# A turn's split products in one run and its transposes, expert products and values in another

## The chip, the cores and the metric

The kernel runs on one core of one Trainium2 chip. The time is that of one execution on the device, in microseconds (us); the figure given for a kernel is the median of its runs. TensorE multiplies matrices and transposes tiles, ScalarE applies functions and copies, VectorE does elementwise work and reductions, GpSimd small elementwise work, and SyncE (SP) issues the DMA transfers. Each engine takes its own instructions in order and waits on semaphores that others raise.

## The reference, cut to what matters

Eight sequences of 512 tokens and 256 features pass two layers. The part in question is the first layer's attention (16 heads of 64) together with its expert network:

```python
q = rmsnorm((xn @ Wq).reshape(B, T, H, D), q_rms_w)
k = rmsnorm((xn @ Wk).reshape(B, T, H, D), k_rms_w)
v = (xn @ Wv).reshape(B, T, H, D)
gate = softplus(einsum('bthd,hd->bht', k, u_n) / sqrt(D))
bias = -dist * omega_eff[head] * gate[b, head, j]          # causal
attn = softmax(q @ k.T / sqrt(D) + bias)
x = x + (attn @ v) @ Wproj + experts(xn)    # 32 experts, 8 tokens of each sequence for each
# experts: h = gelu([merged, 1] @ w1[e]); o = [h, 1] @ w2[e]
```

## The kernel before

The attention runs in 64 **turns**; turn s is one sequence and one pair of heads. The turns are a software pipeline written out by hand: in turn s TensorE makes the **scores** of s, transposes the softmax weights of s - 1 (**p**, ten 128x128 blocks for each of the two heads, turn_p0 and turn_p1), multiplies them with v (**values** of s - 1), turns q, k and the bias terms of s + 1 (turn_q, turn_k, turn_aug) and **projects** s + 2 in four pieces of six products (project(s + 2, 0) to (s + 2, 3)).

Scores and projections are **split products**: each operand is held as a high and a low part in the fp32r type, and three products of parts make one. Transposes, values and the expert products are plain fp32.

Every two turns of four begin an expert (s mod 4 is 0 or 1: `hidden`, its first product, and add_bias), the next two end it (s mod 4 is 2 or 3: `turn_hidden`, `expert_output`). In s mod 4 = 2 ScalarE first computes the Gelu of two experts, with a table load before and one after. After every eighth turn TensorE multiplies a whole sequence with Wproj (L1050), 11.4 us.

All eight PSUM banks are in use: bQ (two, pieces of a projection in turn), bR (three) and bS (three). Scores fill bS and bR; the first head's p goes over bS, the second's over bR; values and expert products take bS[0] and bS[1], turn_hidden takes bS[2], which is also the bank of the third group of p0; q, k and the bias terms are turned in bR. So who has copied what out of a bank decides when the next may write.

The other engines, in a turn, in their order before the change:
- ScalarE: square(s + 1); exps of four score tiles (or Gelu); copies of p0 (groups 0 and 2); **rsqrt**(s + 1), an Ln and an Exp; takes piece 1 of the projection; copies of p1; exps; gate (Exp, Ln); takes piece 2; exps; copy_y; copies of q, k and bias terms; takes piece 3.
- VectorE: **lows**, the reductions of the scores (each raises `maxed`; the last four come after mean_square); takes piece 0; copy_p0; newton_step; copy_p1; copy_hidden; gate_input, norm, gate; divide; and the low parts.
- GpSimd: **augment**(s + 1), six small operations that make the slopes and shifts that turn_aug transposes, from gate's result.

The chain that the text speaks of is: square -> mean_square -> rsqrt -> newton_step -> gate_input and norm -> gate -> augment -> turn_aug -> copy_aug -> scores of the next turn. Lines of the rows: L939 scores, L978 transposes of p, L926 project, L1006 values, L1017 and L1034 expert products, L1025 turn_hidden, L959, L964 and L970 turn_q, turn_k and turn_aug; on ScalarE L1201 the copies of p, L1160 and L1163 the Ln and Exp of rsqrt, L1192 exps, L1175 copy_q; on VectorE L1348 lows, L1293 take_raw, L1304 the first Newton step, L1322 gate, L1388 copy_hidden.

## Time and profile before

| what | us |
|---|---|
| median of 3 runs (lowest to highest) | 1359.23 (1357.82 to 1359.45) |
| span of the profiled execution | 1353.4 |
| TensorE busy in the span | 1309.2 |
| VectorE busy | 1090.3 |
| ScalarE busy | 947.7 |
| GpSimd busy | 190.3 |
| first scores of turn 0 to first scores of turn 63 | 86.9 to 1065.7 |

The span runs from the first to the last instruction of the one execution that was profiled; what lies around it (start and end of the launch) is not in it, so the runs' times are some 6 us longer. A matmul in the trace is shown with its modelled end; consecutive ones overlap, so what a run of them costs is read from start to start. Where rows are merged ("x10"), the time is from the first start to the last end. "[0.67 <-POOL ag L1491]" says how long the engine stood idle before and whose event ended it.

### The profile page before, as it was taken

How to read it: one execution, taken by the hardware profiler on the slowest of the kernel's cores; microseconds unless marked ns; L12 is line 12 of the kernel's file. 1: busy time of each engine (PE TensorE's matmuls, PEld its weight loads, DVE VectorE, ACT ScalarE, POOL GpSimd, SP SyncE). 2: the span in 40 equal slices, each digit the busy share in tenths (PEclk: the TensorE clock that was granted, in tenths of full speed). 3: DMA queues.
4: the chain of work that ended last, by engine and by line, in shares of the span. 5: the costliest groups of instructions: out<-in, count | busy, mean ns of one | idle time of the engine just before them, and what ended most of it. 6: DMA issues, size and time to landing. Idle time of an engine off the chain costs nothing. (4 is left out here: it accounts for less than half of the span.)

```text
span 1353.4 us, 32125 instructions
## 1 busy us (share of the span) xinstructions
PE 1309.2 (97%) x11499; PEld 1103.9 (82%) x11499; DVE 1090.3 (81%) x3337; ACT 947.7 (70%) x2376; POOL 190.3 (14%) x564
## 2 busy tenths in 40 slices
PE   5899999999999999999999999999999799999999
PEld 3688888887978888797888878888888588888888
DVE  6869996999699789969996998799699867777663
ACT  6759885888588678858885887688598724444333
POOL 4512111111011111101111111111111100000000
PEclk8889999999999999999999999999999999999999
DMA  6452231332323222322322233233232322111100
GB/s 216 171 173 88 73 132 59 110 116 74 102 74 131 80 89 87 104 88 88 119 93 92 84 102 109 67 108 103 77 99 72 108 82 62 55 56 55 55 17 32
DMA packets 90831, 125.17 MB, mean 92 GB/s; under 512 B 8761, under 2 KB 77105, under 8 KB 90673
## 3 DMA queue, kind: packets, MB, share of 16 engines
q1 hardware_dynamic: 90352, 123.11, 28.2%
q8 instruction: 93, 1.52, 0.5%
q14 instruction: 66, 0.53, 0.1%
q10 hardware_dynamic: 320, 0.00, 0.0%
HBM read 103.69 MB, written 19.40 MB: 91 GB/s over the span
## 5 line engine op out<-in xcount | busy, mean ns | idle before, releaser
L1192 ACT ACTIVATE prob<-prob,low 128x512 f32<-128x512 f32 (+3 forms) x512 | 280.8, 551 | 115.7 <-DVE low L1348 115.7
L1348 DVE CUSTOM_DVE_ANT_0 prob<-at,mask 128x512 f32<-128x512 f32 (+3 forms) x512 | 219.6, 485 | 10.3 <-PE at L939 10.3
L926 PE MATMUL at<-w_hi,c_lo 128*128 128x386 f32 x512 | 190.1, 371 | 1.5 <-DVE area_raw L1293 1.5
L926 PE MATMUL at<-w_hi,c_hi 128*128 128x386 f32 x512 | 174.3, 340 | 0.0
L926 PE MATMUL at<-w_lo,c_hi 128*128 128x386 f32 x512 | 174.0, 340 | 0.0
L1361 DVE TENSOR_SCALAR prob<-prob,rec 128x512 f32<-128x512 f32 (+3 forms) x512 | 169.3, 394 | 4.5
L978 PE MATMUL at<-ident,prob 128*128 128x128 f32 x1280 | 164.3, 275 | 3.2 <-DVE low L1348 1.8
L1006 PE MATMUL at<-probT,v 128*32 128x512 f32 (+3 forms) x2048 | 152.6, 438 | 3.8 <-DVE probT L1371 2.6
L978 PEld LDWEIGHTS at<-ident,prob 128*128 128x128 f32 x1280 | 142.4, 140 | 10.6 <-DVE yT_lo L1377 1.6
L1006 PEld LDWEIGHTS at<-probT,v 128*32 128x32 f32 x2048 | 67.3, 110 | 89.8 <-issue 80.7
L1201 ACT ACTIVATE probT<-at 128x512 f32<-128x512 f32 (+1 forms) x256 | 130.3, 536 | 4.4 <-PE at L978 1.5
L1479 POOL TENSOR_TENSOR slope<-gl,omega 128x8 f32<-128x8 f32 x64 | 12.8, 200 | 842.8 <-DVE gl L1322 821.9
L1149 ACT ACTIVATE area_raw<-at 128x386 f32<-128x386 f32 x192 | 93.4, 486 | 21.6 <-PE at L926 19.5
L926 PEld LDWEIGHTS at<-w_hi,c_lo 128*128 128x128 f32 x512 | 97.3, 190 | 2.2 <-DVE area_raw L1293 1.8
L926 PEld LDWEIGHTS at<-w_lo,c_hi 128*128 128x128 f32 x512 | 97.6, 191 | 0.1
L926 PEld LDWEIGHTS at<-w_hi,c_hi 128*128 128x128 f32 x512 | 96.8, 189 | 0.0
L1192 ACT ACTIVATION_READ_ACCUMULATOR prob<-prob,low 128x1 f32 x512 | 96.7, 189 | 0.0
L939 PE MATMUL at<-kT_hi,qT_hi 64*128 64x512 f32 (+3 forms) x512 | 86.6, 331 | 6.6 <-ACT kT_hi L1179 6.6
L939 PE MATMUL at<-kT_lo,qT_hi 64*128 64x512 f32 (+3 forms) x512 | 85.1, 326 | 1.5
L939 PE MATMUL at<-kT_hi,qT_lo 64*128 64x512 f32 (+3 forms) x512 | 84.7, 324 | 0.0
L939 PE MATMUL at<-kaug,qaug 64*128 64x512 f32 (+3 forms) x512 | 83.6, 319 | 0.0
L1297 DVE TENSOR_REDUCE ssq<-area_sq 128x16 f32<-128x1024 f32 x64 | 77.7, 1214 | 1.6 <-ACT area_sq L1156 1.6
(254 smaller groups left out, 3195.9 us busy)
## 6 DMA issues: line engine op xcount, KB each, us to landing
area_w<-in_L_ffn_w SPq DMA_DIRECT2D x65, 1024.0 KB, 5.5
bias<-in_L_ffn_w SPq DMA_DIRECT2D x160, 32.0 KB, 4.4
x_in<-in_L_attn_x SPq DMA_DIRECT2D x8, 512.0 KB, 5.5
xr<-in_L_attn_x SPq DMA_DIRECT2D x8, 512.0 KB, 4.6
eo_d<-hidT SPq DMA_DIRECT2D x32, 128.0 KB, 1.8
x_d<-xr SPq DMA_DIRECT2D x8, 512.0 KB, 2.9
area_raw<-x_d SPq DMA_DIRECT2D x8, 512.0 KB, 3.9
out<-area_raw SPq DMA_DIRECT2D x7, 512.0 KB, 3.1
```

Of the source, the lines that this page charges most:

```text
L926: m = eng.matmul(bQ[n % 2][:, 0:W], a[:, (j // HP) % 2, k, n * P:(n + 1) * P], w[:, k, j % HP, :], start=start, stop=(k == KC - 1 and a is ...
L939: m = eng.matmul(bC[i][:, at:at + (c + 1) * P], q[rows, c * P:(c + 1) * P], k[rows, 0:(c + 1) * P], start=ready is k_hi_done, stop=q is qaug)
L978: m = eng.transpose(bP[h][i][:, at:at + P], prob[s % 2][h][:, off[c] + kc * P:off[c] + (kc + 1) * P], ident[:, :])
L1006: m = eng.matmul(bY[rows, kc * P:T], v[:, s % 2, kc, rows], probT[j * E // D][:, offT[kc]:offT[kc + 1]], start=(kc == 0), stop=(kc == NT - 1))
L1149: eng.activation(raw[:, j % 2, n, :], bQ[n % 2][:, 0:W], ACT.Copy).then_inc(raw_A.sem, 1)
L1192: eng.activation(sl, sl, ACT.Exp, scale=-1.0, bias=low[:, i:i + 1], accum_out=den[:, i:i + 1]).then_inc(exp_done.sem, 1)
L1201: eng.activation(probT[h][:, x:y], bP[h][i][:, 0:y - x], ACT.Copy).then_inc(done.sem, 1)
L1297: eng.tensor_reduce(ss[:, :], sq[:, :, :].rearrange("p n (i d) -> p (n i) d", d=D), AX.X, ALU.add).then_inc(ssd.sem, 1)
L1348: eng.tensor_tensor_reduce(out=prob[s % 2][h][:, off[c]:off[c + 1]], in0=bC[i][:, at:at + (c + 1) * P], in1=mask[:, (NT - 1 - c) * P:T], s ...
L1361: p = eng.tensor_scalar(sl, sl, rec[:, k:k + 1], None, ALU.mult)
L1479: eng.tensor_tensor(slope32[:, :, :], gl[:, :, :], omega[:, hp * 2:hp * 2 + 2].unsqueeze(1).to_broadcast([P, NT, 2]), ALU.mult).then_inc(a ...
```

## The change

TensorE's, ScalarE's and VectorE's programs of a turn are written in another order. No instruction is added or taken away.
- TensorE: the scores are followed by pieces 0 and 1 of the projection, then come all twenty transposes of p, the expert product, values, turn_q, turn_k, turn_aug, and then pieces 2 and 3. turn_hidden goes ahead of p0, and the third group of p0 now waits for copy_hidden. expert products go ahead of values.
- ScalarE: all four copies of p together, behind the take of piece 1; rsqrt behind them; the take of piece 2 at the end of the turn.
- VectorE: copy_hidden ahead of the copies of p; both copies of p together ahead of newton_step; take_raw (piece 0) behind gate.

```diff
--- before.py
+++ after.py
@@ -983,6 +983,8 @@
                 def turn_p0(s):
                     eng.wait_ge(p_done.sem, p_done.at(s, 1))
                     for i in range(3):
+                        if i == 2 and ends_in(s + 1) is not None:
+                            eng.wait_ge(hidT_done.sem, hidT_done.at(ends_in(s + 1)))
                         if s + 1 < NTURN:
                             eng.wait_ge(maxed.sem, maxed.at(s + 1, i + 1))
                         turn_p(s, 0, i)
@@ -1019,7 +1021,7 @@
                     p.then_inc(pe_h.sem, 1)
 
                 def turn_hidden(m, s):
-                    eng.wait_ge(pt0_A.sem, pt0_A.at(s - 1))
+                    eng.wait_ge(maxed.sem, maxed.at(s, 3))
                     eng.wait_ge(hid_done.sem, hid_done.at(m // 2))
                     for f in range(NF):
                         p = eng.transpose(bH[:, f * P:(f + 1) * P], hid[:, m % 2, f * P:(f + 1) * P], ident[:, :])
@@ -1102,8 +1104,6 @@
                     else:
                         eng.wait_ge(y_done.sem, y_done.at(s - 2))
                         eng.wait_ge(eo_done.sem, eo_done.at(E - 1))
-                    if s > 0:
-                        turn_p0(s - 1)
                     if s + 2 < NTURN:
                         eng.wait_ge(o_done.sem, o_done.at((s - 1) // HP - 1))
                         project(s + 2, 0)
@@ -1111,19 +1111,18 @@
                     if s + 2 < NTURN:
                         project(s + 2, 1)
                     prepare(s, 1)
-                    if s > 0:
-                        turn_p1(s - 1)
                     if ends_in(s) is not None:
                         turn_hidden(ends_in(s), s)
-                    if s + 2 < NTURN:
-                        project(s + 2, 2)
-                    prepare(s, 2)
                     if s > 0:
-                        values(s - 1)
+                        turn_p0(s - 1)
+                        turn_p1(s - 1)
                     if begins_in(s) is not None:
                         hidden(begins_in(s), s)
                     if ends_in(s) is not None:
                         expert_output(ends_in(s), s)
+                    prepare(s, 2)
+                    if s > 0:
+                        values(s - 1)
                     if s + 1 < NTURN:
                         if s == 0:
                             eng.wait_ge(maxed.sem, maxed.at(0, 8))
@@ -1131,6 +1130,7 @@
                         turn_k(s + 1)
                         turn_aug(s + 1)
                     if s + 2 < NTURN:
+                        project(s + 2, 2)
                         project(s + 2, 3)
                     prepare(s, 3)
                     if 0 < s < NTURN and s % HP == 0:
@@ -1244,18 +1244,17 @@
                     elif s < NTURN:
                         exps(s, 3)
                         exps(s, 1)
-                    if s > 0:
-                        copy_p(s - 1, 0, 0)
-                        copy_p(s - 1, 0, 2)
                     prepare(s, 0)
-                    if s + 1 < NTURN:
-                        rsqrt(s + 1)
                     if s + 2 < NTURN:
                         take_raw(s + 2, 1)
                     prepare(s, 1)
                     if s > 0:
+                        copy_p(s - 1, 0, 0)
+                        copy_p(s - 1, 0, 2)
                         copy_p(s - 1, 1, 0)
                         copy_p(s - 1, 1, 2)
+                    if s + 1 < NTURN:
+                        rsqrt(s + 1)
                     if s % 4 == 2:
                         exps(s, 3)
                         gate(s + 1)
@@ -1264,8 +1263,6 @@
                         exps(s, 2)
                     if s + 1 < NTURN and s % 4 != 2:
                         gate(s + 1)
-                    if s + 2 < NTURN:
-                        take_raw(s + 2, 2)
                     prepare(s, 2)
                     if s < NTURN:
                         exps(s, 0)
@@ -1280,6 +1277,7 @@
                         copy_k(s + 1)
                         copy_aug(s + 1)
                     if s + 2 < NTURN:
+                        take_raw(s + 2, 2)
                         take_raw(s + 2, 3)
                     prepare(s, 3)
                 second.scalar(eng)
@@ -1434,22 +1432,21 @@
                     if s < NTURN:
                         lows(s, 2)
                         lows(s, 0)
-                    if s + 2 < NTURN:
-                        take_raw(s + 2)
+                    if ends_in(s) is not None:
+                        copy_hidden(ends_in(s))
                     prepare(s, 0)
+                    prepare(s, 1)
                     if s > 0:
                         copy_p(s - 1, 0)
-                    prepare(s, 1)
+                        copy_p(s - 1, 1)
                     if s + 1 < NTURN:
                         newton_step(s + 1)
-                    if s > 0:
-                        copy_p(s - 1, 1)
-                    if ends_in(s) is not None:
-                        copy_hidden(ends_in(s))
                     if s + 1 < NTURN:
                         gate_input(s + 1)
                         norm(s + 1)
                         gate(s + 1)
+                    if s + 2 < NTURN:
+                        take_raw(s + 2)
                     if s < NTURN:
                         divide(s, 0)
                     if begins_in(s) is not None:
```

TensorE, in the middle of a turn that begins an expert, before, from the second head's transposes of p (L978) over a piece of the projection (L926) and values (L1006) to the expert product (L1017):

```order
L978 MATMUL at<-ident,prob 128x128 x10
L926 MATMUL at<-w_hi,c_lo 128x386
L926 MATMUL at<-w_lo,c_hi 128x386
L926 MATMUL at<-w_hi,c_hi 128x386
L926 MATMUL at<-w_hi,c_lo 128x386
L926 MATMUL at<-w_lo,c_hi 128x386
L926 MATMUL at<-w_hi,c_hi 128x386
L1006 MATMUL at<-probT,v 32x512 x4
L1006 MATMUL at<-probT,v 32x384 x4
L1006 MATMUL at<-probT,v 32x256 x4
L1006 MATMUL at<-probT,v 32x128 x4
L1017 MATMUL at<-area_w,tok 32x256 x8
```

The same place after the change (L1019 is `hidden`, L1008 values), up to the first product of the third piece:

```order
L926 MATMUL at<-w_hi,c_hi 128x386
L978 MATMUL at<-ident,prob 128x128 x20
L1019 MATMUL at<-area_w,tok 32x256 x8
L1008 MATMUL at<-probT,v 32x512 x4
L1008 MATMUL at<-probT,v 32x384 x4
L1008 MATMUL at<-probT,v 32x256 x4
L1008 MATMUL at<-probT,v 32x128 x4
L959 MATMUL at<-ident,area_sq 128x128 x4
L964 MATMUL at<-ident,area_sq 128x128 x4
L970 MATMUL at<-ident,ag 68x128 x4
L926 MATMUL at<-w_hi,c_lo 128x386
L926 MATMUL at<-w_lo,c_hi 128x386
```

The piece that stood between the transposes and values has gone behind turn_aug (L970), where twelve products of L926 now stand ahead of the scores instead of six.

ScalarE in such a turn, before, from the second exps to the take of piece 2 (lnv and r are rsqrt; area_raw<-at is a take of a piece; probT<-at a copy of p; ge and gp are gate):

```order
L1192 ACTIVATE prob,dens<-prob,low 128x256 x2
L1201 ACTIVATE probT<-at 128x512
L1201 ACTIVATE probT<-at 128x384
L1160 ACTIVATE lnv<-ssq 128x16
L1163 ACTIVATE r<-lnv 128x16
L1149 ACTIVATE area_raw<-at 128x386
L1201 ACTIVATE probT<-at 128x512
L1201 ACTIVATE probT<-at 128x384
L1192 ACTIVATE prob,dens<-prob,low 128x384 x2
L1168 ACTIVATE ge<-ge 128x8
L1170 ACTIVATE gp<-ge 128x8
L1149 ACTIVATE area_raw<-at 128x386
```

After:

```order
L1192 ACTIVATE prob,dens<-prob,low 128x256 x2
L1149 ACTIVATE area_raw<-at 128x386
L1201 ACTIVATE probT<-at 128x512
L1201 ACTIVATE probT<-at 128x384
L1201 ACTIVATE probT<-at 128x512
L1201 ACTIVATE probT<-at 128x384
L1160 ACTIVATE lnv<-ssq 128x16
L1163 ACTIVATE r<-lnv 128x16
L1192 ACTIVATE prob,dens<-prob,low 128x384 x2
L1168 ACTIVATE ge<-ge 128x8
L1170 ACTIVATE gp<-ge 128x8
L1192 ACTIVATE prob,dens<-prob,low 128x128 x2
```

The two instructions of rsqrt moved from ahead of the second head's copies to behind them.

VectorE in a turn that ends an expert, after the change, behind its last reduction of the scores (L1346), up to divide:

```order
L1346 ISA prob,low<-at,mask 128x128
L1346 ISA low 128x1
L1386 COPY hidT<-at 128x256
L1369 COPY probT<-at 128x384 x2
L1302 SCALAR_TENSOR_TENSOR nw<-r 128x16
L1304 TENSOR_TENSOR nw<-nw,ssq 128x16
L1306 SCALAR_TENSOR_TENSOR rs<-nw,r 128x16
L1314 TENSOR_TENSOR gl<-area_raw,rs 128x8
L1316 SCALAR_TENSOR_TENSOR ge<-gl 128x8
L1324 TENSOR_TENSOR area_sq<-area_raw,rs 128x1024
L1320 SCALAR_TENSOR_TENSOR gl<-gl,gp 128x8
L1291 COPY area_raw<-at 128x386
```

copy_hidden (L1386) stood behind the second copy of p before, and the take of piece 0 (L1291) ahead of the first.

## Rows read from the trace of the kernel before

**Rows 1.** The page: span, busy time, granted clock in 40 slices, the group of p transposes.

```profile
span 1353.4 us, 32125 instructions
...
PE 1309.2 (97%) x11499; PEld 1103.9 (82%) x11499; DVE 1090.3 (81%) x3337; ACT 947.7 (70%) x2376; POOL 190.3 (14%) x564
...
PEclk8889999999999999999999999999999999999999
...
L978 PE MATMUL at<-ident,prob 128*128 128x128 f32 x1280 | 164.3, 275 | 3.2 <-DVE low L1348 1.8
```

**Rows 2.** The waits of TensorE, 200 to 1000 us: total, times, longest.

```profile
PE at L939 <- ACT kT_hi L1179: 4.0, 12, 0.5
```

**Rows 3.** The timeline of TensorE, turn 36: start, duration, engine, line, operation.

```profile
645.27 0.50 PE L939 MATMUL at<-kT_hi,qT_hi 64*128 64x512 f32 x2
...
647.99 1.31 PE L978 MATMUL at<-ident,prob 128*128 128x128 f32 x10
649.06 0.42 PE L926 MATMUL at<-w_hi,c_lo 128*128 128x386 f32 x1
649.32 0.34 PE L926 MATMUL at<-w_lo,c_hi 128*128 128x386 f32 x1
...
651.27 1.25 PE L978 MATMUL at<-ident,prob 128*128 128x128 f32 x10
...
657.68 0.60 PE L970 MATMUL at<-ident,ag 128*68 128x128 f32 x4
...
659.29 0.50 PE L939 MATMUL at<-kT_hi,qT_hi 64*128 64x512 f32 x2
```

**Rows 4.** The timeline of TensorE, first scores of turns 34 and 35.

```profile
616.15 0.50 PE L939 MATMUL at<-kT_hi,qT_hi 64*128 64x512 f32 x2
...
630.67 0.50 PE L939 MATMUL at<-kT_hi,qT_hi 64*128 64x512 f32 x2 [0.31 <-ACT kT_hi L1179]
```

**Rows 5.** The timeline of ScalarE in turn 36: rsqrt, copies of p1, exps.

```profile
650.79 0.21 ACT L1160 ACTIVATE lnv<-ssq 128x16 f32<-128x16 f32 x1
651.09 0.22 ACT L1163 ACTIVATE r<-lnv 128x16 f32<-128x16 f32 x1
...
651.91 1.15 ACT L1201 ACTIVATE probT<-at 128x512 f32<-128x512 f32 x2
652.95 0.61 ACT L1192 ACTIVATE prob<-prob,low 128x384 f32<-128x384 f32 x1
```

**Rows 6.** The timeline of turn 35: copy_q on ScalarE and VectorE's low part after it.

```profile
643.50 0.69 ACT L1175 ACTIVATE qT_hi<-at,q_scale 128x512 fp32r<-128x512 f32 x1 [0.83 <-PE at L959]
...
644.22 0.75 DVE L1333 SCALAR_TENSOR_TENSOR qT_lo<-at,q_scale,qT_hi 128x512 fp32r<-128x512 f32 x1 [0.32 <-ACT qT_hi L1175]
```

**Rows 7.** The timeline of VectorE in turn 0: take_raw, first Newton step, gate.

```profile
92.88 0.55 DVE L1293 COPY area_raw<-at 128x386 f32<-128x386 f32 x1
93.35 0.16 DVE L1304 SCALAR_TENSOR_TENSOR nw<-r 128x16 f32<-128x16 f32 x1
...
95.39 0.16 DVE L1322 SCALAR_TENSOR_TENSOR gl<-gl,gp 128x8 f32<-128x8 f32 x1
```

**Rows 8.** The timeline of TensorE: turn_aug of turn 0 and the first scores of turn 1.

```profile
97.49 0.63 PE L970 MATMUL at<-ident,ag 128*68 128x128 f32 x4 [0.67 <-POOL ag L1491]
...
99.11 0.49 PE L939 MATMUL at<-kT_hi,qT_hi 64*128 64x512 f32 x2
```

**Rows 9.** The timeline of turn 34: VectorE's gate and the last operation of augment.

```profile
625.88 0.16 DVE L1322 SCALAR_TENSOR_TENSOR gl<-gl,gp 128x8 f32<-128x8 f32 x1
...
627.52 0.21 POOL L1491 TENSOR_TENSOR ag<-shift,ag 128x8 fp32r<-128x8 f32 x1
```

**Rows 10.** The timeline of VectorE: copy_hidden in turn 35, first instruction behind lows in turn 36.

```profile
639.25 0.41 DVE L1388 COPY hidT<-at 128x256 f32<-128x256 f32 x1
...
651.36 0.56 DVE L1293 COPY area_raw<-at 128x386 f32<-128x386 f32 x1
```

**Rows 11.** Windows around turn 63: busy time of each engine, granted clock, DMA share.

```profile
1076.00:1079.50 3.50, 3.11 (x20) 1.05 (x24) 2.56 (x8) 1.60 (x7) 0.00 (x0) 0.51 0.00 0
```

## The prediction

> **What bounds the kernel now.** I read the page first: TensorE is busy 97% of the 1353.4 us span [rows 1]. "Busy" says little where matmuls are pipelined, so the second view is the list of waits, TensorE's own, in the stretch from 200 to 1000 us: in 800 us it waited 4.0 us in total [rows 2]. In these turns TensorE never stands still for long, so a turn lasts as long as its matmuls take. The other engines have slack, and what counts is how much of it a new order uses up.
>
> The third view is the timeline of a turn, from one first score product to the next [rows 3]: 645.27 to 659.29, 14.02 us, a turn that begins an expert (s mod 4 is 0 or 1). The turns that end one take 14.52 (616.15 to 630.67, the one with Gelu) and 14.60 (630.67 to 645.27) [rows 4]. I give times below from the turn's first score product.
>
> **The meant gain: fewer changes of kind.** Before, split products and plain fp32 work alternate three times a turn; after, once. What does a change cost? In [rows 3] the ten transposes begin at 647.99. A transpose follows the last one by 0.109 us (the run of ten lasts 1.25, one alone 0.275 [rows 1, 3]; nine steps are between), 0.16 after the first, so the tenth begins at about 649.03. The second product after it begins at 649.32, 0.29 later: one transpose step and one product step (0.109 + 0.177; the latter from 649.32 to 651.27, 11 steps). So the entry costs about nothing, and the exit into the transposes is one of these 11 equal steps. The first product's own step of 0.26 (649.06 to 649.32) against 0.177 bounds it from above: 0.08 an entry, two entries fewer in 61 turns, 10 us at most. Below nothing I have no reason for. I take 0, the value that the starts on both sides support. The changes between products on 128 rows, the scores on 64 and the 32-column products stay as many as they were.
>
> **The cost: the next turn's chain starts later and has one product piece more behind it.** It runs: last transpose of p1, ScalarE's copy of it, Ln and Exp of rsqrt (which the change puts behind all four copies), VectorE's Newton steps, gate input, norm and gate, GpSimd's six operations of augment, TensorE's turn_aug, then now two pieces of project instead of one, then the scores. Step by step for a turn that begins an expert:
> - Scores take 2.72 (645.27 to 647.99), the two pieces of project 2.21 (649.06 to 651.27) [rows 3]. So p0 begins at 4.93, and the last of the 20 transposes at 4.93 + 19 x 0.109 = 7.00. Before, the first p1 transpose began at 651.27 - 645.27 = 6.00, so p1 stands where it did, and p0 lies later.
> - From the last transpose's start to ScalarE's next instruction behind the copy: 652.95 - (651.27 + 9 x 0.109) = 0.70 [rows 3, 5]. Ln at 7.70. In the old order Ln came at 650.79 - 645.27 = 5.52, ahead of p1. This is the move that counts.
> - Ln to Exp 0.30, Exp 0.22 [rows 5], hop to VectorE 0.03 (643.50 + 0.69 to 644.22 [rows 6]): Newton at 8.25.
> - Newton to gate, with gate input and norm between, 2.04 (93.35 to 95.39) [rows 7]: gate at 10.29. These rows are from the first turn, the only place where TensorE already waits for augment: gate to turn_aug is 95.39 to 97.49, 2.10 [rows 7, 8]. While VectorE's big multiplications ran beside it, GpSimd was slower; in the turn at 616 VectorE stood idle first, and gate to GpSimd's last end was 627.73 - 625.88 = 1.85 [rows 9], 1.88 with a hop of 0.03. After the change a copy from PSUM (take_raw) stands behind gate, ahead of the multiplications. I take 1.95, nearer to the short one, and keep both. turn_aug at 12.24.
> - turn_aug to the scores with one piece behind it is 1.62 (97.49 to 99.11) [rows 8], one more piece is 6 x 0.177 = 1.06: next scores at 14.92. Before 14.02: **+0.90**.
>
> Does TensorE come earlier than 12.24? Before, from the end of p1 (651.27 + 10 x 0.109 = 652.36) to turn_aug (657.68) it took 5.32 with one piece in it, so without it 4.26: 7.11 + 4.26 = 11.37. It waits some 0.9 us before turn_aug, with the two pieces and the scores queued behind it. turn_q, eight transposes earlier (11.37 - 8 x 0.109 = 10.50), needs norm, which ends as gate starts, at 10.3: no wait of its own. The old turn_aug began at 657.68 - 645.27 = 12.41, so it hardly moves: the old slack of the chain paid for the later rsqrt, and the piece behind it is then bare.
>
> **Turns that end an expert.** turn_hidden now stands ahead of p0: 2 x 0.109 = 0.22. The third group of p0 waits for VectorE's copy of the hidden values (one PSUM bank). VectorE gets to it after the turn's last score reduction, 651.36 - 645.27 = 6.09; the copy takes 0.41, hop 0.03: 6.53 [rows 3, 10]. The group would be due at 4.93 + 0.22 + 7 x 0.109 = 5.91. A stall of 0.62, and all behind it later by 0.84: 15.76. Against 14.52 and 14.60: **+1.24** and **+1.16**. If VectorE is done sooner the stall could vanish; that is the low bound, 30 x 0.62 = 19 us. The Gelu turn has a second suspect: its scores already wait 0.31 for copy_k [rows 4], so copy_k ends at about 14.5. The exps ahead of it started when the p1 copies ended, at 7.8 (651.91 + 1.15 - 645.27 [rows 5]); now they start behind rsqrt, at 7.70 + 0.84 + 0.52 = 9.06. That puts copy_k at 15.8, less the take of a piece that has gone behind it: on the edge of 15.76, so I add nothing, and 0.2 in 15 turns for the range.
>
> **What costs nothing.** VectorE's and ScalarE's takes of the third piece move to the turn's end, where only the piece after next needs their bank. Values wait for all four copies, which end at 7.8; TensorE stands at 7.1 then with an expert's products between, which cover them. If they did not, values would be 0.7 late. The expert products run earlier in the turn; their weights are issued by the same SP instructions at a turn's end or start, a turn ahead, and the SP queue passes nothing new.
>
> **The sum.** Turns 1 to 61 carry all of it: 31 x 0.90 = 27.9, 15 x 1.24 = 18.6, 15 x 1.16 = 17.4. Turn 0 has no transposes of p; its chain begins 0.47 earlier (92.88 to 93.35, the copy ahead of Newton goes [rows 7]) and gets 1.06 behind it, less 0.15 for GpSimd: 0.5. The last turns have no projections; I put 0. Total 64.4: span 1353.4 to about 1418, and the median of the runs, which stands 5.8 above the profiled span, 1359.2 to **1424 us**.
>
> **Rivals.**
> - The gain is real and the wait is not (faster). If an entry costs the full 0.08 and the chain fits in TensorE's work, the time is 1359 - 10 = 1349. It decides if p1's last transpose to turn_aug takes under 11.37 - 7.00 = 4.4 us; the rows add up to 5.2. I see no hop that is 0.8 too long. 0.07 with all ways of being faster.
> - The wait is smaller than worked out, 1362 to 1395: half of the 0.9, no stall on the hidden copy. 0.06.
> - Nothing changes, since both are small: 0.02.
> - The clock falls. Transposes are now 20 or 22 in one run and twelve more stand around the new wait. The granted clock reads 9, so nine tenths or more, in each slice of the turns before [rows 1], but in 1076 to 1079.5, after a stretch of transposes with short waits, it was 0.51 [rows 11], which is 1.2 GHz. If each turn had such a stretch, 3.5 us at half the speed would lose up to 1.7 us, 61 times: 1424 + 104 = 1528. In the stretch before the fall there were several runs and three waits in 6 us; here some 2 us of transposes stand between products. 0.04.
> - The forecast, with its own range 1404 to 1442: 0.81.
>
> The Trainium skill, TensorE: Matmul & The Clock Gate, Part 4 (PE-mode transpose), says that transposes do not count as work for the clock as other matmuls do. By that rule the long run of transposes is the wrong thing to make, and the case of the falling clock would be the likeliest. The turns before, with 32 transposes in each and no slice of a lower clock, give it little room.
>
> **How the numbers follow.** The range: gate to turn_aug between 1.88 and 2.10 is -4 to +9 us, no hidden stall -19, copy_k +3, entries dearer than nothing -10, and 0.15 a turn for hops put together, +-9; not all at once, so 1404 to 1442. It leaves out the clock, most of the smaller wait and the faster cases, and the ends of my own: 2 in 10. This kernel's runs differ by 0.1%, so 0.2% is about what can be told from no change. Slower by more than that: 0.81 + 0.06 + 0.04 = 0.91; within 0.02; faster 0.07.
>
> **What would show it.** TensorE's waits should show turn_aug waiting for GpSimd's last augment operation in every turn, 0.8 to 1.1 us; waits at the third group of p0 for the hidden copy in 30 turns; turns of 14.9 and 15.8. Steps of products and transposes unchanged, clock 1.00. I am wrong if turns take under 14.0 (then changes of kind cost more than the starts show), or if the first wait is elsewhere, most likely at turn_q for norm or at the scores for copy_k.

## The result, and the profile after the change

The change makes the kernel slower: 1431.02 us (median of 4 runs, 1426.0 to 1434.0) against 1358.53 (4 runs, 1350.47 to 1359.45), a ratio of 1.0566 [1.0529, 1.0604]. This ratio and those below, each with its 95% interval, are the estimates on record and not the quotient of the two medians beside them, which would be 1.0534 here. The profiled execution spans 1429.6 us against 1353.4 [rows 1], so 76.2 more.

The page of the changed kernel, with the rows that answer to [rows 1] and the one of turn_aug (busy time, mean ns of one, idle time before and what ended most of it):

```profile
span 1429.6 us, 32157 instructions
...
PE 1330.6 (93%) x11499; PEld 1104.8 (77%) x11499; DVE 1100.6 (77%) x3337; ACT 973.4 (68%) x2376; POOL 193.3 (14%) x564
...
PEclk9799999999999999999999999999999989999999
...
L978 PE MATMUL at<-ident,prob 128*128 128x128 f32 x1280 | 158.8, 276 | 18.1 <-DVE hidT L1386 16.3
...
L970 PE MATMUL at<-ident,ag 128*68 128x128 f32 x256 | 40.6, 282 | 48.7 <-POOL ag L1488 48.7
```

The matmuls are the same 11499, and so are the counts of the other engines; the 32 instructions that the total has more are none of these. TensorE's share of the span fell from 97% to 93%; what is new is idle time ahead of two groups. The waits of TensorE from 200 to 1000 us, as in [rows 2] (total, times, longest):

```profile
PE at L970 <- POOL ag L1488: 37.0, 47, 0.9
PE at L978 <- DVE hidT L1386: 11.2, 24, 0.6
...
```

The first stands in every turn of the stretch, 47 in all, the second in each of its 24 turns that end an expert. The wait for copy_k, all that [rows 2] had, is not in the list any more. Now the timeline of TensorE in turn 33, which begins an expert (start, duration, tiles; compare [rows 3]):

```profile
642.23 0.50 PE L939 MATMUL at<-kT_hi,qT_hi 64*128 64x512 f32 x2
...
647.14 2.35 PE L978 MATMUL at<-ident,prob 128*128 128x128 f32 x20
649.42 1.07 PE L1019 MATMUL at<-area_w,tok 128*32 128x256 f32 x16
650.30 2.34 PE L1008 MATMUL at<-probT,v 128*32 128x512 f32 x32
652.65 0.66 PE L959 MATMUL at<-ident,area_sq 128*128 128x128 f32 x4
653.14 0.60 PE L964 MATMUL at<-ident,area_sq 128*128 128x128 f32 x4
654.53 0.63 PE L970 MATMUL at<-ident,ag 128*68 128x128 f32 x4 [0.79 <-POOL ag L1488]
...
657.21 0.50 PE L939 MATMUL at<-kT_hi,qT_hi 64*128 64x512 f32 x2
```

The turn lasts 14.98 us. turn_aug (L970) begins 1.88 after turn_q (652.65 to 654.53); in the turn of [rows 3] these two stand 0.93 apart. So the wait costs 0.95 from start to start, though 0.79 is listed: the listed figure counts from the modelled end of the matmul before. The chain that it waits for, in the same turn, on ScalarE (copies of p, Ln, Exp), then VectorE (first Newton step, gate), then GpSimd (last of augment):

```profile
647.84 2.18 ACT L1201 ACTIVATE probT<-at 128x512 f32<-128x512 f32 x4
649.91 0.21 ACT L1160 ACTIVATE lnv<-ssq 128x16 f32<-128x16 f32 x1
650.21 0.22 ACT L1163 ACTIVATE r<-lnv 128x16 f32<-128x16 f32 x1
```

```profile
650.46 0.18 DVE L1302 SCALAR_TENSOR_TENSOR nw<-r 128x16 f32<-128x16 f32 x1 [0.70 <-ACT r L1163]
...
652.51 0.16 DVE L1320 SCALAR_TENSOR_TENSOR gl<-gl,gp 128x8 f32<-128x8 f32 x1
```

```profile
654.15 0.33 POOL L1488 TENSOR_TENSOR ag<-shift,ag 128x8 fp32r<-128x8 f32 x1
```

VectorE stood idle for 0.70 before the Newton steps, so it was ScalarE's late Exp that set them; from there on each step of the chain began within 0.1 us of the end of the one before it. Then the two turns that end an expert, TensorE again: turn 34 (Gelu) from 657.21, turn 35 behind it from 672.86.

```profile
662.39 0.93 PE L978 MATMUL at<-ident,prob 128*128 128x128 f32 x7
663.68 1.64 PE L978 MATMUL at<-ident,prob 128*128 128x128 f32 x13 [0.37 <-DVE hidT L1386]
...
670.18 0.63 PE L970 MATMUL at<-ident,ag 128*68 128x128 f32 x4 [0.61 <-POOL ag L1488]
...
672.86 0.50 PE L939 MATMUL at<-kT_hi,qT_hi 64*128 64x512 f32 x2
...
678.26 0.93 PE L978 MATMUL at<-ident,prob 128*128 128x128 f32 x7
679.79 1.64 PE L978 MATMUL at<-ident,prob 128*128 128x128 f32 x13 [0.60 <-DVE hidT L1386]
...
686.47 0.63 PE L970 MATMUL at<-ident,ag 128*68 128x128 f32 x4 [0.79 <-POOL ag L1488]
...
689.16 0.50 PE L939 MATMUL at<-kT_hi,qT_hi 64*128 64x512 f32 x2
```

Both have two waits each; they last 15.65 and 16.30. After seven transposes of p the eighth, which is in the third group, waits for the copy of the hidden values. VectorE in turn 35, its first score reduction and that copy:

```profile
674.70 0.68 DVE L1346 CUSTOM_DVE_ANT_0 prob<-at,mask 128x512 f32<-128x512 f32 x1
...
679.32 0.42 DVE L1386 COPY hidT<-at 128x256 f32<-128x256 f32 x1
```

Not every such pair of turns is split like this one: in 7 of the 15 Gelu turns, turn_aug begins 2.16 behind gate instead of 1.84, they last 15.97 or more, and the turn behind them mostly 15.95 to 15.98. From turn 22 on the two together take 31.93 to 31.96 either way. In turn 34 GpSimd's fourth operation of augment took 0.21 and VectorE's four multiplications beside it 1.80; in turn 42, one of the longer ones, 0.51 and 1.41.

Turn 0 became longer by 1.3: 13.53 (86.37 to 99.90) for 12.25 (86.86 to 99.11). TensorE there, GpSimd's last operation of augment, and the windows of its transposes and of all full turns (busy time of PE, PEld, DVE, ACT and POOL, granted clock, DMA share, GB/s):

```profile
94.69 1.09 PE L959 MATMUL at<-ident,area_sq 128*128 128x128 f32 x4 [2.25 <-DVE area_sq L1324]
```

```profile
96.10 0.33 POOL L1488 TENSOR_TENSOR ag<-shift,ag 128x8 fp32r<-128x8 f32 x1
```

```profile
94.60:98.00 3.40, 3.31 (x15) 2.99 (x16) 3.37 (x10) 1.78 (x4) 2.29 (x8) 0.51 0.67 269
148.00:1125.00 977.00, 918.05 (x8618) 753.78 (x8620) 788.39 (x2494) 739.43 (x1899) 128.55 (x435) 1.00 0.28 88
```

With no values to make yet and the third piece gone behind, TensorE waited 2.25 us for norm, and the transposes after that wait ran at a granted clock of 0.51, the lower level of 1.2 GHz. In the full turns the clock is 1.00.

**The whole in one table.** The length of a turn is read from first score product to first score product, and is the mean over turns 4 to 61; "begin" are the turns that begin an expert and carry no output product, "output" those with the product of a sequence, "Gelu" s mod 4 = 2, "behind" s mod 4 = 3. The sum runs from the first scores of turn 1 to those of turn 62. The kernels e1 to e9 are the experiments below.

| kernel | begin | output | Gelu | behind | sum of turns 1 to 61 |
|---|---|---|---|---|---|
| before | 13.99 | 25.37 | 14.53 | 14.61 | 951.2 |
| after | 14.98 | 26.34 | 15.82 | 16.17 | 1024.8 |
| e1, rsqrt early | 14.18 | 25.53 | 15.01 | 15.71 | 980.8 |
| e2, piece 2 ahead | 14.02 | 25.91 | 15.54 | 15.53 | 985.5 |
| e3, hidden copy early | 14.98 | 26.32 | 15.35 | 15.80 | 1012.0 |
| e5 = e1 + e3 | 14.20 | 25.52 | 14.59 | 15.29 | 968.6 |
| e8 = e1 + e2 + e3 | 14.00 | 25.94 | 14.69 | 15.09 | 965.2 |
| e4, before with more changes of kind | 13.99 | 25.37 | 14.71 | 14.64 | 954.5 |
| e7, before with rsqrt late | 13.98 | 25.29 | 14.97 | 14.61 | 958.8 |
| e6, before with take 2 late | 13.99 | 25.37 | 14.15 | 14.61 | 945.5 |
| e9, e6 with exps late | 13.99 | 25.37 | 14.11 | 14.49 | 942.9 |

Of the 76.2 us, 73.7 stand in turns 1 to 61, 1.3 in turn 0, 0.5 in turn 62, 1.3 behind that, and the start took 0.5 less.

### The profile page after: what moved, and what is told of

Same layout as the page of the kernel before. It is cut to its first block and busy times, and to the rows that moved or that the text cites. A ratio compares the mean times of both kernels' runs of the same rounds, so it can differ in the third digit from the quotient of the medians.

```text
span 1429.6 us, 32157 instructions
## 1 busy us (share of the span) xinstructions
PE 1330.6 (93%) x11499; PEld 1104.8 (77%) x11499; DVE 1100.6 (77%) x3337; ACT 973.4 (68%) x2376; POOL 193.3 (14%) x564
## 5 line engine op out<-in xcount | busy, mean ns | idle before, releaser
L1346 DVE CUSTOM_DVE_ANT_0 prob<-at,mask 128x512 f32<-128x512 f32 (+3 forms) x512 | 220.1, 486 | 28.5 <-PE at L939 28.4
L926 PE MATMUL at<-w_hi,c_lo 128*128 128x386 f32 x512 | 185.6, 362 | 0.0
L978 PE MATMUL at<-ident,prob 128*128 128x128 f32 x1280 | 158.8, 276 | 18.1 <-DVE hidT L1386 16.3
L926 PE MATMUL at<-w_hi,c_hi 128*128 128x386 f32 x512 | 173.9, 340 | 0.0
L926 PE MATMUL at<-w_lo,c_hi 128*128 128x386 f32 x512 | 173.5, 339 | 0.0
L978 PEld LDWEIGHTS at<-ident,prob 128*128 128x128 f32 x1280 | 143.6, 142 | 27.1 <-DVE hidT L1386 23.9
L1201 ACT ACTIVATE probT<-at 128x512 f32<-128x512 f32 (+1 forms) x256 | 135.3, 545 | 35.5 <-PE at L978 31.9
L1008 PE MATMUL at<-probT,v 128*32 128x512 f32 (+3 forms) x2048 | 151.3, 436 | 0.0
L1008 PEld LDWEIGHTS at<-probT,v 128*32 128x32 f32 x2048 | 68.1, 110 | 84.6 <-issue 64.7
L1369 DVE COPY probT<-at 128x384 f32<-128x384 f32 x128 | 70.7, 554 | 43.4 <-PE at L978 42.7
L926 PEld LDWEIGHTS at<-w_hi,c_lo 128*128 128x128 f32 x512 | 96.6, 189 | 4.6
L926 PEld LDWEIGHTS at<-w_lo,c_hi 128*128 128x128 f32 x512 | 96.9, 189 | 0.1
L926 PEld LDWEIGHTS at<-w_hi,c_hi 128*128 128x128 f32 x512 | 96.5, 188 | 0.0
L970 PE MATMUL at<-ident,ag 128*68 128x128 f32 x256 | 40.6, 282 | 48.7 <-POOL ag L1488 48.7
```

The lines of the kernel that those rows point to most:

```text
L926: m = eng.matmul(bQ[n % 2][:, 0:W], a[:, (j // HP) % 2, k, n * P:(n + 1) * P], w[:, k, j % HP, :], start=start, stop=(k == KC - 1 and a is ...
L970: m = eng.transpose(bR[2][0:AG, n * P:(n + 1) * P], ag[:, n, :].bitcast(F32), ident[:, :])
L978: m = eng.transpose(bP[h][i][:, at:at + P], prob[s % 2][h][:, off[c] + kc * P:off[c] + (kc + 1) * P], ident[:, :])
L1008: m = eng.matmul(bY[rows, kc * P:T], v[:, s % 2, kc, rows], probT[j * E // D][:, offT[kc]:offT[kc + 1]], start=(kc == 0), stop=(kc == NT - 1))
L1201: eng.activation(probT[h][:, x:y], bP[h][i][:, 0:y - x], ACT.Copy).then_inc(done.sem, 1)
L1346: eng.tensor_tensor_reduce(out=prob[s % 2][h][:, off[c]:off[c + 1]], in0=bC[i][:, at:at + (c + 1) * P], in1=mask[:, (NT - 1 - c) * P:T], s ...
```

## The experiments

**Is it the late rsqrt?** e1 takes the changed kernel and puts rsqrt back ahead of the take of piece 1 and of ScalarE's copies of p; VectorE's order stays as changed.

```diff
                     prepare(s, 0)
+                    if s + 1 < NTURN:
+                        rsqrt(s + 1)
...
                         copy_p(s - 1, 1, 2)
-                    if s + 1 < NTURN:
-                        rsqrt(s + 1)
```

> The changed kernel with one edit: on ScalarE the Ln and Exp of rsqrt stand ahead of the take of piece 1 and of the four copies of p again. My theory (the chain to turn_aug is late because rsqrt waits for the last p1 copy, and it ends bare in front of two pieces): the chain then starts when VectorE has made its second copy of p, at about 7.5 us instead of 8.25 of a turn, and TensorE's wait at turn_aug falls from 0.8 to about 0.1 us; turns that begin an expert go from 14.98 to about 14.2, those that end one lose some 0.7 too; 1385 us in all (1378 to 1395). Rival (the long runs themselves cost, by the clock or by TensorE's steps): at most a few us are won, 1425 to 1431. Rival (VectorE, not ScalarE, holds the chain): Newton starts no earlier, 1431.

Measured: 1386.57 us (1381.67 to 1396.1), ratio 1.0256 [1.0193, 1.0319] to a before of 1353.09 in that comparison. TensorE's waits from 200 to 1000 us:

```profile
PE at L978 <- DVE hidT L1386: 11.7, 24, 0.6
```

The listed wait for augment is gone from all turns. It is not quite gone in time: TensorE in its turn 36,

```profile
675.28 0.66 PE L959 MATMUL at<-ident,area_sq 128*128 128x128 f32 x4
...
676.43 0.63 PE L970 MATMUL at<-ident,ag 128*68 128x128 f32 x4
```

turn_aug begins 1.15 after turn_q; in the kernel before, which also has plain fp32 work just ahead of turn_q, it is 0.93. So 0.22 is left, and the turns that begin an expert last 14.18, 0.19 more than before. Moving rsqrt back saves 44.0 of the 73.7 us; whether it is rsqrt's place alone that costs them, this run can't say.

**Is it the bare piece?** e2 leaves rsqrt late and puts piece 2 ahead of turn_q, where it covers the chain (VectorE's take_raw goes behind copy_hidden, so that piece 2 finds its bank free).

```diff
                         values(s - 1)
+                    if s + 2 < NTURN:
+                        project(s + 2, 2)
...
                         turn_aug(s + 1)
                     if s + 2 < NTURN:
-                        project(s + 2, 2)
                         project(s + 2, 3)
```

> The changed kernel with piece 2 of the projection ahead of turn_q (behind values) instead of behind turn_aug, and VectorE's take of piece 0 behind copy_hidden, which piece 2 needs; rsqrt stays late. My theory: the piece covers the wait at turn_aug, which falls from 0.8 to under 0.1 us, and turns that begin an expert go from 14.98 to 14.1; 1378 us (1370 to 1390). There is one more change of kind a turn; if those cost the upper bound of 0.08 us it is 5 us more. Rival (rsqrt's place alone makes the loss, whatever stands behind turn_aug): the wait at turn_aug stays and little is won, over 1415.

Measured: 1388.78 us (1385.19 to 1392.09), ratio 1.026 [1.0213, 1.0306]. Its waits from 200 to 1000 us:

```profile
PE at L978 <- DVE hidT L1387: 12.7, 24, 0.6
PE at L939 <- ACT kT_hi L1180: 6.2, 12, 0.8
PE at L1052 <- ACT area_raw L1150: 1.8, 6, 0.3
```

Turns that begin an expert are back at 14.02, with rsqrt as late as in the changed kernel. Putting the piece back saves 39.3 us, though rsqrt stays where it is. So the savings of e1 and e2 are not two shares of the loss: they take away the same wait, and the 0.98 needs both, a late chain and a piece that has left the place where it covered it. (A bare piece with the chain early still costs 0.19, as e1 shows.) What the changed kernel's longer Gelu turn hid comes up: the scores wait for copy_k, the prediction's second suspect, and the output product for a take on ScalarE.

**Is the late rsqrt alone harmful?** e7 is the other half: the kernel before with ScalarE's rsqrt behind its last copy of p, and VectorE's Newton steps behind both copies. TensorE's order is untouched.

```diff
-                    if s + 1 < NTURN:
-                        rsqrt(s + 1)
                     if s + 2 < NTURN:
                         take_raw(s + 2, 1)
...
                         copy_p(s - 1, 1, 2)
+                    if s + 1 < NTURN:
+                        rsqrt(s + 1)
```

> The kernel before with one part of the change alone: rsqrt behind all four copies of p on ScalarE and newton_step behind both copies on VectorE; TensorE's order is untouched. My theory (the late rsqrt only uses up the chain's slack; what costs is that the piece which covered it now stands behind turn_aug): gate at 10.3 us of a turn, turn_aug possible at 12.25 while TensorE comes at 12.4: turns stay within 0.1 us, 1353 to 1360. Rival (the late rsqrt alone costs what the change costs): 50 us more.

Measured: 1362.74 us (1356.9 to 1367.83), ratio 1.0062 [1.0033, 1.0091] to 1355.78. The turns that begin an expert do not move (13.98). Its waits from 200 to 1000 us, and the scores behind a Gelu turn:

```profile
PE at L939 <- ACT kT_hi L1179: 9.0, 12, 1.0
```

```profile
636.28 0.49 PE L939 MATMUL at<-kT_hi,qT_hi 64*128 64x512 f32 x2 [0.72 <-ACT kT_hi L1179]
```

Of the 7.6 us that the sum of turns rose, 6.9 stand in the 15 Gelu turns, where ScalarE reaches copy_k later still, and 1.3 in turn 3; the turns that begin an expert are 0.7 shorter together. The median lies above the 1353 to 1360 that I expected: I had not counted what the late rsqrt does to copy_k. For the turns that begin an expert it settles the prediction's sentence that the old slack of the chain paid for the later rsqrt: it did, and only the bare piece turned it into a wait.

**The hidden copy.** e3 lets VectorE copy the hidden values two reductions earlier, in the changed kernel.

```diff
                         lows(s, 2)
-                        lows(s, 0)
                     if ends_in(s) is not None:
                         copy_hidden(ends_in(s))
+                    if s < NTURN:
+                        lows(s, 0)
```

> The changed kernel with VectorE's copy_hidden ahead of the last two score reductions instead of behind them. My theory: TensorE's wait at the third group of p0 (0.37 and 0.60 us shown in the two turns that end an expert) nearly vanishes, and since the chain to turn_aug hangs on p1, all of it comes off these turns: 30 x 0.5 = 15 us, 1416 (1411 to 1422); turns that begin an expert stay at 14.98. Rival (the wait is only passed on, to the p1 groups that need the last reductions, or to turn_aug): 1428 to 1431.

Measured: 1416.42 us (1414.84 to 1420.6), ratio 1.0473 [1.0428, 1.0519]. Its waits:

```profile
PE at L970 <- POOL ag L1489: 36.8, 48, 0.9
PE at L978 <- DVE hidT L1386: 1.2, 7, 0.2
```

The stall at the third group fell from 11.2 to 1.2 in the list, the Gelu turn by 0.47 and the turn behind it by 0.37; the wait for augment stays.

**Do the two add up?** e5 has the edits of e1 and e3 together.

> The changed kernel with both edits, rsqrt early on ScalarE and copy_hidden ahead of the last two reductions. My theory (two separate losses, one in every turn, one in the turns that end an expert): the gains add, 1386 less 15: 1371 us (1365 to 1378). Rival (both take from the same slack): 1380 or more.

Measured: 1374.05 us (1372.74 to 1378.93), ratio 1.0136 [1.0094, 1.0178]. In sums of turns 1 to 61, e1 saves 44.0 and e3 12.8, together 56.8; e5 saves 56.2. They add up, so they are two waits at two places and not one that moves about.

**What is a change of kind worth?** e4 is the kernel before with the transposes of p cut into their groups and half pieces of the projection between them: six entries into split products in a turn instead of three, 183 more in turns 1 to 61.

```diff
+                    if mixed:
+                        turn_p0(s - 1, (0,))
...
+                        project(s + 2, 0, (0,))
+                        turn_p0(s - 1, (1,))
+                        project(s + 2, 0, (1,))
+                        turn_p0(s - 1, (2,))
+                        project(s + 2, 1, (0,))
+                        turn_p1(s - 1, (0,))
+                        project(s + 2, 1, (1,))
+                        turn_p1(s - 1, (1, 2))
```

> The kernel before with the same instructions, but the groups of p0 and the first of p1 alternate with halves of pieces 0 and 1: six entries from fp32 work into split products a turn instead of three, and six exits. 183 more of each in all. My theory (a change of kind costs nothing, by the starts on both sides): 1358 us, within 4. Rival (an entry costs the 0.08 us that its first product's step shows): 15 us more, 1373. If it were still more, the change's idea would be right and its price hidden by the new waits.

Measured: 1357.47 us (1351.2 to 1360.11), ratio 1.0029 [1.0002, 1.0055] to 1353.09. The turns that begin an expert last 13.99 as before. TensorE in one of them (L981 transposes of p, L928 project):

```profile
645.67 0.66 PE L981 MATMUL at<-ident,prob 128*128 128x128 f32 x4
646.08 0.42 PE L928 MATMUL at<-w_hi,c_lo 128*128 128x386 f32 x1
646.34 0.34 PE L928 MATMUL at<-w_lo,c_hi 128*128 128x386 f32 x1
646.52 0.34 PE L928 MATMUL at<-w_hi,c_hi 128*128 128x386 f32 x1
646.70 0.49 PE L981 MATMUL at<-ident,prob 128*128 128x128 f32 x3
646.94 0.42 PE L928 MATMUL at<-w_hi,c_lo 128*128 128x386 f32 x1
```

Three transposes (646.70 to 646.94) take 0.24, so 0.08 each where the step in a run is 0.109, and the first product behind them has a step of 0.26 where the next have 0.18. What the entry seems to cost is given back at the exit before it. Three more entries in a turn cost nothing that these turns show; the 3.3 us that the sum rose are in the Gelu turns (14.71), where copy_k is waited for longer (6.2 us in the list for 4.0).

**And with all the waits mended?** e8 is the changed kernel with e1's, e2's and e3's edits: one change of kind fewer in each turn than before, and no late chain.

> The changed kernel with all three: rsqrt early, piece 2 ahead of turn_q, copy_hidden early. Two runs of each kind a turn instead of three before, and none of the new waits. My theory (changes of kind are free): turns as before, 14.0, and 14.5 to 14.7 where an expert ends; within 5 us of the kernel before. Rival (a change of kind costs 0.08 us or more): 5 us or more faster than before, 0.996 and below.

Measured: 1365.27 us (1361.37 to 1376.54), ratio 1.007 [1.0043, 1.0098] to 1355.78. Its waits, and the third group of p0 in its turn 35:

```profile
PE at L1052 <- ACT area_raw L1150: 2.4, 7, 0.3
PE at L978 <- DVE hidT L1387: 2.0, 11, 0.2
```

```profile
650.39 0.93 PE L978 MATMUL at<-ident,prob 128*128 128x128 f32 x7
651.50 1.64 PE L978 MATMUL at<-ident,prob 128*128 128x128 f32 x13 [0.18 <-DVE hidT L1387]
```

The turns that begin an expert are at 14.00, those of before at 13.99: longer runs of one kind bring nothing even when nothing is late. I had expected the whole within 5 us of before, and it is 9.5 off by the medians, 14.0 by the sum of turns. Two rests make up nearly all of the 14.0. In the turns that end an expert, 15 x (0.16 + 0.48) = 9.6, the third group still comes late: in turn 35 the 13 transposes begin 1.11 behind the seven, where 7 x 0.109 = 0.76 would do, so 0.35 is lost, and in the Gelu turn 0.22 in the same way. And the seven output turns have 0.57 more each, 4.0, with the wait for a take on ScalarE in them.

**Mending the wait that the kernel before had.** The trace of before has one wait in its turns [rows 2], for copy_k in the Gelu turn. e6 lets ScalarE take piece 2 behind copy_aug there.

```diff
-                    if s + 2 < NTURN:
+                    if s + 2 < NTURN and s % 4 != 2:
                         take_raw(s + 2, 2)
...
                     if s + 2 < NTURN:
+                        if s % 4 == 2:
+                            take_raw(s + 2, 2)
                         take_raw(s + 2, 3)
```

> The kernel before with one edit: in the turns with a Gelu, ScalarE takes piece 2 of the projection behind its copies of q, k and the bias terms instead of ahead of the last exps, as the changed kernel does in every turn. There the scores of the next turn waited for copy_k (0.31) and then for VectorE's low parts. My theory: ScalarE's copies come 0.4 us earlier, the waits at the scores vanish, and the Gelu turn and the one behind it lose some 0.3 us each, 15 times: 5 to 9 us, 0.995 of before. Rival (ScalarE is late by its exps whatever the take's place): within 0.1%.

Measured: 1349.44 us (1343.32 to 1352.79), ratio 0.9952 [0.9926, 0.9979] to 1355.78. The Gelu turn went from 14.53 to 14.15 and TensorE has no wait listed from 200 to 1000 us. It ran a second time beside e9:

> The same kernel as with the late take of piece 2 alone, on the same chip as the one with both edits: 0.995 of before again, turns of 14.12 and 14.61.

Measured: 1350.51 us (1344.03 to 1356.15), and a before of 1350.46 in that comparison: ratio 1.000 [0.9977, 1.0022]. The turns are the same as the first time, so the kernel's own share is the 5.7 us of the sum of turns; the rest of a run varies more than that (last section). From the ratios alone, faster than before is not settled for e6: the second comparison does not bear the first out.

e9 adds to e6 that in Gelu turns ScalarE's last exps go behind copy_aug.

```diff
-                    if s < NTURN:
+                    if s < NTURN and s % 4 != 2:
                         exps(s, 0)
...
                         copy_aug(s + 1)
+                    if s < NTURN and s % 4 == 2:
+                        exps(s, 0)
```

> The kernel before with the late take of piece 2 in the Gelu turns and, in the same turns, ScalarE's last two exps behind its copies of q, k and the bias terms. What is left in the turn behind the Gelu turn (14.61 against 14.0 + 0.22 for turn_hidden) is the scores' third product waiting for VectorE's low part of k, which comes after ScalarE's copy of y. My theory: copy_y, copy_q and copy_k come some 0.6 us earlier, the low parts with them, and that turn goes from 14.61 to about 14.3: 4 to 5 us on top of the 6 of the late take, 0.992 of before. Rival (VectorE has no room: its own queue sets the low parts): the turn stays at 14.6 and the ratio at 0.995.

Measured: 1342.58 us (1339.46 to 1354.99), ratio 0.9946 [0.9918, 0.9974] to 1350.46. The turn behind Gelu fell from 14.61 to 14.49, less than the 14.3 hoped for. Its scores hardly wait any more, and p0 begins 0.33 earlier than in e6 (2.83 for 3.16 in turn 35), but half of that is lost at values, which begin 0.44 behind the last product ahead of them, for 0.27 in e6. The sum of turns is 8.3 us below before's. This kernel has the lowest median and the shortest turns of the study. Its ratio rests on one comparison, as e6's first did; what speaks for it beyond that is the sum of turns.

## Why the prediction was right, and where a size was off

1424 was forecast, 1404 to 1442, and 1431.02 came; slower, by the two waits that were named, at the two places named. The mechanism was right; that the number came so near is in part luck, some 4 us of it (see the step from span to median). By its steps:

- **Changes of kind are free.** Right: three more in a turn leave it at 13.99 (e4), one fewer at 14.00 (e8). The upper bound of 0.08 an entry would have been 0.24 for e4's turn, and is excluded.
- **The chain of a turn that begins an expert.** Forecast p0 at 4.93, Ln 7.70, gate 10.29, turn_aug 12.24, next scores 14.92; turn 33 shows 4.91, 7.68, 10.28, 12.30 and 14.98. The one step that was chosen between two rows, gate to turn_aug, was put at 1.95 and is 2.02 (652.51 to 654.53), nearer to the long end. The term measures 31 x 0.98 = 30.4 us for 27.9. e1 and e2 show that it was the late rsqrt and the bare piece together, as argued, and e7 that the first alone costs these turns nothing.
- **The hidden copy.** The mechanism is right (e3 takes it away); this is the mis-sized term of the sum. I had 15.76 for both turns, from VectorE's reductions ending 6.09 after the first scores. That figure came from turn 36, which begins an expert. It fits the Gelu turn: in turn 34 the eighth transpose stands 0.53 late (662.39 + 7 x 0.109 = 663.15, it began at 663.68), for 0.62, and the turn lasts 15.65. It does not fit the turn behind it, where VectorE still divides until 1.84 after the first scores (674.70 - 672.86), so the reductions end at 6.46 (679.32 - 672.86), and the eighth transpose begins at 6.93 (679.79 - 672.86), where I had 6.53. The turn lasts 16.30. With 15.82 and 16.17 as means, the pair is 2.85 longer than before, 15 x 2.85 = 42.8 us for the 36.0 forecast. The trace of before had the figure. In its turn 35, which began at 630.67 [rows 4], VectorE's first instruction behind the reductions is this one, 6.68 into the turn:

```profile
637.35 0.55 DVE L1293 COPY area_raw<-at 128x386 f32<-128x386 f32 x1
```

With 6.68 for 6.09 the forecast of that turn would have been 0.59 longer, 16.35. The end of the reductions has to be read in each kind of turn.
- **copy_k** as the second suspect: it was put at 15.8, less the take behind it, and in turn 34 it ends at 15.29, 0.36 ahead of the next scores, so it costs nothing there. It comes out once the chain's wait is gone (e2).
- **Turn 0** was put at 0.5 and is 1.3. The chain was right: turn_aug begins at 10.12 (96.49 - 86.37), before at 10.63 (97.49 - 86.86), and with 1.06 more behind it that makes 0.55. What I left out is the clock. TensorE waited at turn_q for 2.25 us, and the granted clock was 0.51 behind that wait. The slow turn_q and turn_k (begun at 94.69 and 95.57) cost nothing of their own, since turn_aug had to wait for augment, which ended at 96.43. But from turn_aug to the next scores it took 3.41 (96.49 to 99.90), where turn 33 takes 2.68 at full clock (654.53 to 657.21): 0.73. The rival of the falling clock is what happened here, once, and in none of the turns 1 to 61.
- **From span to median.** I added 5.8 for what lies around the span, and the section on the time before says the same. The changed kernel's profiled execution took 1431.36 for a span of 1429.6, so 1.8 lies around it, and 1.7 to 1.9 in every other run that has both figures. By that the profiled execution of before took about 1355, and the other 4 is its distance from the median of the three timed runs. The sum was 64.4 and the span grew by 76.2: 9.8 short in turns 1 to 61 and 2 in the ends. Without the 4 us the forecast would have been 1420, so this error brought it nearer to the result, by luck. The prediction also says that the kernel's runs differ by 0.1%; over 27 runs they differ by 1.0% (last section).
- **The rivals.** No gain was real; the smaller wait did not come; the clock kept its level in the turns (1.00 from 148 to 1125 us) with runs of 20 transposes between products in each. The Trainium skill's rule, TensorE: Matmul & The Clock Gate, Part 4 (PE-mode transpose), that transposes do not count for the clock as other matmuls do, does not decide this kernel's time; the trace shows no lower clock in its turns.

## What to carry to other kernels

When work is moved along an engine's order, ask what it covered where it stood: here six products between a late chain and the scores were worth 1 us a turn, and putting them back gave it back though the chain stayed late. A slack chain and a covering piece are one reserve, and an edit that spends both needs to be added up along the whole chain, in every kind of turn and not in one. Sorting matmuls by kind to save changes is worth nothing when their start-to-start steps on both sides of a change add up to the plain ones.

## What the runs showed of the hardware that was not expected

Runs of one kernel lie up to 14 us apart (before: 1347.65 to 1361.71 in 27 runs), while the mean lengths of the turns repeat within 0.01 us in two profiled executions of e6, and each of turns 1 to 61 within 0.06. What differs most from one profiled execution to another is the part ahead of the turns; within one kernel's runs only the mean granted clock is on record, 0.997 in the shortest of those 27 runs and 0.984 in the longest. The first 80 us of e6 and of e9 (busy times, granted clock, DMA share, GB/s):

```profile
0.00:80.00 80.00, 59.48 (x378) 46.62 (x379) 61.64 (x177) 53.78 (x113) 36.57 (x77) 0.94 0.53 183
```

```profile
0.00:80.00 80.00, 59.64 (x323) 46.34 (x324) 54.41 (x165) 49.76 (x103) 34.54 (x69) 0.83 0.51 178
```

The same code got through 378 matmuls in one and 323 in the other; turn 0 begins at 81.35 and 89.94. At 0.89 (before) it is 86.86, at 0.79 (e5) 90.06, at 0.77 (e8) 92.92. Why the clock is granted so differently there stays open. For a difference of a few us the turns are to be compared, not the totals: e9's profiled execution spans 1348.3 and e6's 1342.3, though e9's turns are the shorter ones by 2.6 us.
